# Running both rounds of a recurrent scan layer together: two alternating chains to level 63, then one chain over 64 images

## The reference, cut to what matters

```
for ci, ni, nm, nc in spiral:                 # 1024 steps
    local = g[:, ci, :]
    neigh = (g[:, ni, :] * nm).sum(axis=1) / nc     # up to four neighbours
    u     = concat([local, neigh])                  # 256 values
    y     = tanh(u @ w1 + b1) @ w2 + b2             # 256 hidden units, one number
    g[:, ci, :] = local + y * w_y
```

## Time and profile before

| | us |
|---|---|
| median of 3 runs | 5175.27 (5174.68 to 5177.31) |
| the profiled execution | 5175.03 |
| its span, first to last instruction | 5173.2 |
| PE busy | 4980.8 (96%) |
| VectorE busy | 3493.7 (68%) |
| ScalarE busy | 2927.9 (57%) |
| GpSimd busy | 1018.0 (20%) |
| mean granted clock of TensorE | 0.976 |

### The profile page before, as it was taken

One profiled execution on the slowest core, in us unless ns is written; L12 is line 12 of the kernel. 1 busy time (PEld: TensorE's weight loads), 2 busy tenths in 40 slices (PEclk: granted clock), 3 DMA queues, 4 the chain that ended last, 5 costly groups with the idle time before them and its releaser, 6 DMA issues.

```text
span 5173.2 us, 57594 instructions
## 1 busy us (share of the span) xinstructions
PE 4980.8 (96%) x18384; PEld 2468.8 (48%) x18384; DVE 3493.7 (68%) x6954; ACT 2927.9 (57%) x5457; POOL 1018.0 (20%) x3424
## 2 busy tenths in 40 slices
PE   8998998899999999999999999999999998998997
PEld 3565466344444444444444444444444443565466
DVE  6885886666666666666666666666666656885886
ACT  2222222677777777777777777777777762222222
POOL 4432441011111111111111111111111113432441
PEclk9998998899999999999999999999999999998998
DMA  7653331111111111111111111111111107653331
GB/s 167 93 84 59 47 47 34 38 41 41 41 39 40 41 41 41 41 41 41 41 41 41 41 41 41 41 41 41 41 41 41 41 29 162 93 86 59 47 47 34
DMA packets 373022, 273.22 MB, mean 53 GB/s; under 512 B 338672, under 2 KB 339952, under 8 KB 372720
## 3 DMA queue, kind: packets, MB, share of 16 engines
q1 hardware_dynamic: 372720, 269.54, 22.2%
HBM read 135.29 MB, written 134.22 MB: 52 GB/s over the span
## 4 chain that ended last, share of the span: by engine, by line
PE 91%; DVE 4%; ACT 3%; DMA 1%; issue 1%; POOL 0%; SPq 0%; DVEq 0%; POOLq 0%; ACTq 0%
PE psum L809 35%; PE psum L762 11%; PE psum L782 8%; PE psum L745 8%; PE psum L755 8%; PE psum L844 5%; PE psum L831 5%; PE psum L795 5%; PE psum L859 3%; PE psum L820 3%; ACT hidden L690 2%; DVE near L585 1%; DVE near L562 1%; DVE near L564 1%; POOL near L449 0%
## 5 line engine op out<-in xcount | busy, mean ns | idle before, releaser
L809 PE MATMUL psum<-probs,v 128*128 128x512 f32 x4096 | 1966.9, 603 | 1.3 <-DVE x L653 1.3
L611 DVE TENSOR_REDUCE top<-psum 128x1 f32<-128x1024 f32 x1024 | 1253.5, 1224 | 996.9 <-PE psum L795 996.9
L697 ACT ACTIVATE probs<-psum 128x512 f32<-128x512 f32 x2048 | 1110.3, 594 | 453.4 <-PE psum L782 449.4
L702 ACT ACTIVATE psum<-psum,top 128x1024 f32<-128x1024 f32 x1024 | 1113.0, 1087 | 354.5 <-DVE top L611 354.4
L690 ACT ACTIVATE hidden<-psum,b_col 128x160 f32<-128x160 f32 (+15 forms) x976 | 457.6, 492 | 1296.6 <-PE psum L755 1280.6
L809 PEld LDWEIGHTS psum<-probs,v 128*128 128x128 f32 x4096 | 718.2, 190 | 764.7 <-issue 509.1
L449 POOL TENSOR_TENSOR near<-arena 128x32 f32<-128x32 f32 (+9 forms) x1440 | 597.2, 444 | 1102.2 <-PE psum L755 984.8
L762 PE MATMUL psum<-hidden,w2wy 128*128 128x160 f32 (+14 forms) x1952 | 606.1, 435 | 54.7 <-ACT hidden L690 41.4
L755 PE MATMUL psum<-near,w_sum 128*128 128x160 f32 (+14 forms) x1952 | 583.9, 423 | 60.3 <-POOL near L449 33.6
L745 PE MATMUL psum<-arena,w_own 128*128 128x32 f32 (+15 forms) x2192 | 583.4, 395 | 34.4 <-DMA arena<-x_cells 18.5
L461 POOL TENSOR_TENSOR ratio<-shrink,total 128x8 f32<-128x8 f32 x128 | 26.0, 203 | 2896.8 <-ACT shrink L713 2896.8
(11 more groups left out here) (64 smaller groups left out, 3359.6 us busy)
## 6 DMA issues: line engine op xcount, KB each, us to landing
x<-layer_out SPq DMA_DIRECT2D x128, 512.0 KB, 3.2
layer_out<-x SPq DMA_DIRECT2D x128, 512.0 KB, 2.6
arena<-x_cells SPq DMA_DIRECT2D x6, 1920.0 KB, 19.0
layer_out<-arena SPq DMA_DIRECT2D x6, 1920.0 KB, 17.0
arena<-layer_out SPq DMA_DIRECT2D x6, 1920.0 KB, 18.2
y_cells<-arena SPq DMA_DIRECT2D x6, 1920.0 KB, 16.9
arena<-x_cells SPq DMA_DIRECT2D x4, 2000.0 KB, 19.0
layer_out<-arena SPq DMA_DIRECT2D x4, 2000.0 KB, 15.9
```

The costliest lines, as they stand in the source:

```text
L611: nc.vector.reduce_max(top[i % 2][:, m:m + 1], rows_ps[m % 2][:], AX_X, negate=True).then_inc(row_max, 1)
L697: nc.scalar.activation(probs[u % PROBS][:], keys_ps[u % 2], ACT.Exp).then_inc(probs_ready, 1)
L702: nc.scalar.activation(rows_ps[m % 2][:], rows_ps[m % 2][:], ACT.Exp, bias=top[i % 2][:, m:m + 1], accum_out=total[i % 2][:, m:m + 1]).the ...
L809: nc.tensor.matmul(mix_ps, v[i % 2][:, tile(t)], probs[u % PROBS][:], start=(m == 0), stop=(m == MT - 1)).then_inc(mixed, 1)
```

## The change

Both rounds of a layer are one pass. To level 63 (`JOIN` = 64) there are two streams, A (images 0 to 31) and B (32 to 63), whose levels alternate on every engine; from level 64 there is one stream, BOTH, with 64 images. Each stream has its own semaphores. A and B have one PSUM buffer each for the pre-activations and one for the steps; BOTH alternates between two. The steps of A and B gain a wait for the update of the level before.

The arena has 64 images but only 528 cells: 16 ending cells and the first 32 stay for good, and a window of 480 cells is refilled. The chunks are now at most 96 cells: first levels 0, 2, 8, 14, 20, 27, 34, 43, 53, 65, 80, 101. Chunks 0 to 5 and the ending cells are loaded at the start. Chunks 6 to 11 take places whose earlier tenants must have been stored and read for the last time, which is after levels 13, 26, 33, 40, 40 and 49; they are first read at levels 27, 36, 46, 58, 73 and 94. Every load and store is made twice, for A and for B. For the second scan layer A's first loads are issued in attention after job 116 (`EARLY`), B's at its end.

`near` and `hidden` are twice as large and share their memory with attention's `v` and `probs`; attention starts and ends with a wait for that. The three `scan(n)` in the diff are, in order, those of GpSimd, VectorE and TensorE. The first image load of attention waits for all stores of images 0 to 31, which now end with the layer.

```diff
+JOIN = 64
+A, B, BOTH = range(3)
+SPAN = {A: range(JOIN), B: range(JOIN), BOTH: range(JOIN, LEVELS)}
+PICTURES = {A: slice(0, IMAGES), B: slice(IMAGES, BATCH), BOTH: slice(0, BATCH)}
+CHUNK = 96
+WINDOW = 5 * CHUNK
...
-    arena = sb("arena", [P, IMAGES, CELLS])
+    arena = sb("arena", [P, BATCH, ARENA])
+    shared = [sb(f"shared{n}", [P, BATCH * WIDE]) for n in range(4)]
...
+        def load(n, g, k):
+            for e in earlier_tenants(k):
+                sp.wait_ge(stored[g][e], 16 * (n + 1))
+                wait_level(g, n, max(LAST_READ[chunk_cells(e)]))
...
+            first_loads(0, A)
             load_scan_weights(1)
+            first_loads(0, B)
             load_heads()
-            for r in range(GROUPS):
-                scan(r, r + 1 < GROUPS)
+            follow(0)
...
+                if j == EARLY:
+                    first_loads(1, A)
...
+        def scan(n):
+            for lv in range(LEVELS):
+                for c in streams_at(lv):
+                    late_sums(n, c, lv)
...
+        def scan(n):
+            for c in (A, B):
+                sums(n, c, 1)
+            for lv in range(JOIN - 1):
+                for c in (A, B):
+                    add_steps(n, c, lv + 1)
+                    update(n, c, lv)
+                    if lv + 2 < JOIN:
+                        sums(n, c, lv + 2)
+            sums(n, BOTH, JOIN)
+            add_steps(n, BOTH, JOIN)
+            for c in (A, B):
+                update(n, c, JOIN - 1)
+            for lv in range(JOIN, LEVELS):
+                if lv + 1 < LEVELS:
+                    sums(n, BOTH, lv + 1)
+                    add_steps(n, BOTH, lv + 1)
+                update(n, BOTH, lv)
...
+        def steps(n, c, lv):
+            if c != BOTH:
+                positive(pe, updated[c], levels_done(n, c, lv - 1))
...
+        def scan(n):
+            for c in (A, B):
+                own_products(n, c, 0)
+                near_products(n, c, 0)
+            for lv in range(JOIN):
+                for c in (A, B):
+                    steps(n, c, lv)
+                    if lv + 1 < JOIN:
+                        own_products(n, c, lv + 1)
+                        near_products(n, c, lv + 1)
+            own_products(n, BOTH, JOIN)
+            for lv in range(JOIN, LEVELS):
+                near_products(n, BOTH, lv)
+                steps(n, BOTH, lv)
+                if lv + 1 < LEVELS:
+                    own_products(n, BOTH, lv + 1)
```

More of the change, by code:

```diff
@@ L68, in wavefront @@
     order = sorted(level, key=lambda c: (c in ending, level[c], ring[c]))
[L69 to L73, removed]
+    return rank, level, ending, order
+RANK, LEVEL, ENDING_CELLS, ORDER = levels_of_cells()
@@ new lines, with chunk_levels, chunk_cells @@
+LEVELS = max(LEVEL.values()) + 1
+STARTS = [sum(LEVEL[c] < lv and c not in ENDING_CELLS for c in ORDER) for lv in range(LEVELS + 1)]
+OWN_LEVEL = [LEVEL[c] for c in ORDER]
+CHUNK = 96
+WINDOW = 5 * CHUNK
+def chunk_levels():
+    first = [0, 2]
+    for lv in range(2, LEVELS):
+        if STARTS[lv + 1] - STARTS[first[-1]] > CHUNK and lv > first[-1]:
+            first.append(lv)
+    return first + [LEVELS]
+CHUNKS = chunk_levels()
+ENDING = len(CHUNKS) - 1
+def chunk_cells(k):
+    return slice(STARTS[-1], CELLS) if k == ENDING else slice(STARTS[CHUNKS[k]], STARTS[CHUNKS[k + 1]])
@@ L120, in wavefront @@
         edges.append([(n, k, count) for count, n, k, _, _ in ops[EDGE]])
[L121 to L139, removed]
+    grid = np.array([y * SIDE + x for y, x in ORDER])
+    return grid, ends, sums_late, sums_old, sums_new, steps, edges, first_read, last_read
+GRID, ENDS, SUMS_LATE, SUMS_OLD, SUMS_NEW, STEPS, EDGES, FIRST_READ, LAST_READ = wavefront()
 def level_size(lv):
     return STARTS[lv + 1] - STARTS[lv] + (ENDS[lv] is not None)
-def chunk_cells(k):
-    return slice(STARTS[-1], CELLS) if k == ENDING else slice(STARTS[CHUNKS[k]], STARTS[CHUNKS[k + 1]])
 def positive(engine, semaphore, value):
@@ L589, in update @@
[L589 to L600 removed]
+                for e in STREAMS if c == BOTH else (c,):
+                    if lv - 2 in SPAN[e]:
+                        dve.wait_ge(updated[e], levels_done(n, e, lv - 2))
@@ new lines, in update @@
+        def update(n, c, lv):
+            dve.wait_ge(step_ready[c], levels_done(n, c, lv))
+            for o, w, place in own_parts(lv):
+                own = arena[:, PICTURES[c], place:place + w]
+                ins = nc.vector.scalar_tensor_tensor(own, columns(step(c, lv), c, lv, o, w), b2wy[n][:], own,
+                                                     ALU.add, ALU.add)
+            ins.then_inc(updated[c], 1)
+        def scan(n):
[12 more added lines that the diff above has]
+            for lv in range(JOIN, LEVELS):
@@ L673, in _ @@
         prepare_scan(0)
-        for r in range(GROUPS):
-            scan(r)
+        scan(0)
         prepare_heads()
@@ L889, in _ @@
         pe.wait_ge(out_ready, 2 * JOBS)
-        for r in range(GROUPS, 2 * GROUPS):
-            scan(r)
+        scan(1)
 def build(nc, t):
```

353 lines of the change are left out of this document (182 added, 171 removed).

## The result

The changed kernel takes **4949.8 us** (median of 4 runs, 4948.88 to 4950.95) against 5175.6 us of the kernel before; the ratio is 0.956, 95% interval 0.9547 to 0.958. The forecast was 4916, its range 4870 to 4995. The gain is 225.8 us where 259 were forecast.

A forecast was written before the change was run, and what follows sets the result against it. TensorE looks 96% busy, but the prediction saw time lost in scan waits, narrow levels and gaps. Terms 37 - 49.5 - 42 - 206 + 2 - 1 = -259.5 took 5175.0 to 4916 us; range 4870 to 4995.

The forecast's parts named there:

- What bounds the kernel: Whole kernel: TensorE's 96% busy hides waits within scan levels; narrow levels and the gap between rounds lose time, attention stays.
- a): Levels 64 to 121 run once over 64 images instead of twice over 32: 200 us a layer, gain 206.
- I take the rows of equal columns: Merged levels: a level of w cells is priced by the period of an old level of 2w cells.
- b): Gap between the two rounds of each scan layer disappears: gain 49.5 us.
- c): First layer's start: level 1 waits for the second stream's third load, starting at about 69.6 instead of 32.92: cost 37.
- d): Second layer's start: B's loads land 1 us sooner than the present 29; early loads in attention cost nothing: -1.
- e): Levels 1 to 63 as two alternating chains: the wait for tanh goes, 256.5 for 266.9 us, gain 42.
- f): Refill and hand-over to attention: refills off the path, four short stores replace two, +2 us; kernel end 0.
- Refill stalls: Rival, wide levels: second stream's loads or small descriptors hold them up too, three stalls a layer: 5036 us; chance 0.05.
- Merged levels bound by VectorE as a whole: Rival, merged levels: VectorE's operations take twice the time for twice the elements, 233 for 199 us: 4984; chance 0.10.
- Mutual exclusion: Rival, levels 1 to 63: VectorE and GpSimd exclude each other, +100 x 4 us if fully serial: 5318, slower; chance 0.03.
- the second rival: Merged levels: VectorE bounds them if its operations take twice the time, 4984 us; chance 0.10.

The follow-up runs named there:

- third_addition: Changed kernel with every step addition of the merged levels beyond the first two left out of the computation: 4936.5 us, -13.3 against the changed kernel.
- align: Changed kernel with only the chunks' places in the arena moved by one or two cells each: 4937.8 us, -12.0 against the changed kernel.
- load_order: Changed kernel; in the first layer both streams' chunk 0, ending cells and chunk 1 load first, the second layer's weights last: 4921.7 us, -28.1.
- no_alternation: Changed kernel with levels 0 to 63 of stream A run first, then those of B, then the merged levels: 4992.2 us, +42.4.
- combined_early: Changed kernel with wait order, load order, chunk places and shorter last stores changed, plus B's second-layer first loads mostly issued during attention job 124: 4870.7 us.

## Why the prediction was right, point by point

- **What bounds the kernel**: right. The gains came from the scan, from narrow levels and from gaps, none from attention.
- **a)** The mechanism was right, the term was mis-sized: 200 a layer forecast, 211.2 measured. "I take the rows of equal columns" holds at 7 cells (4.75 forecast and measured) and not below. By sizes, forecast and measured sums are 38.0 and 39.2 at 7 cells, 33.4 and 35.0 at 6, 46.5 and 50.0 at 5, 33.0 and 37.1 at 4, 21.8 and 24.3 at 3, 19.2 and 21.0 at 2; the 1.75 for ending cells is not in these. The failing step is that an old level of equal columns had two additions, a merged one from level 92 on has three, and I added 0.15 for that at 3 cells only; third_addition prices one at about 0.25. The 6-cell levels also met unlucky places (align, 1.7 to 3.3 a layer), and the order of the waits cost 0.03 to 0.09 in most levels from 91 on. With two additions and lucky places 5 cells still took 3.70 for 3.58 and 4 cells 3.14 for 3.00; these 0.12 to 0.14 a level stay unexplained.
- **b)** Right: 49.5, no idle stretch at mid-layer.
- **c)** Right, and load_order shows its cause: 38.2 measured for 37, 28 of which are only issue order.
- **d)** Right: 29.0. The early loads in attention cost nothing, attention being 3364.2 for 3364.0. no_alternation (10.7 us without B) and combined_early (19.5) show what most of those 29 us are: the wait for B's three loads.
- **e)** 46.5 for 42. The three groups of sizes took 113.6, 64.1 and 76.5 a stream where 113.9, 65.0 and 77.5 were forecast. At 9 cells a turn takes 2.97 to 3.01 in the plain levels, below the 3.15 to 3.25 forecast, and 3.18 only in the mean with the dearer ones. The forecast's sum of the old chain, 266.9, stands 1.0 above the 265.9 of the trace: the forecast of 256.5 was worth 38, so the gain was missed by some 9, not 4. "What goes is the wait for tanh" fits the rows: from the neighbour products to the steps it is 1.79 here, 1.88 in the earlier trace rows and 1.99 in no_alternation.
- **f)** Failed: costs of 8.1 and 9.5 where 2 and 0 stood. The step counted four short stores as if bytes decided; instead twice as many runs, half of them with an end that is no multiple of 32 bytes, took 22.4 us from the last update to the end for nearly the bytes that took 12.9.
- **Rivals.** Refill stalls: none, no PE wait for `arena` after level 1. Merged levels bound by VectorE as a whole (4984): false, VectorE is busy 165 of 211 us; but its third addition is on the path at the narrow end, a small part of that rival. Mutual exclusion: false as a rival for the time, but it is there in single instructions. The prediction took 230 us for VectorE where the earlier trace rows have 213, so the overlap that it found in the kernel before is 66 and not 83. In the changed kernel VectorE is busy 425.8 and GpSimd 241.1 of 508.4 us, and the sums of busy time are those of two rounds before (425.1 and 238.0). But an instruction that is held up counts as busy. These are the same sums of GpSimd and VectorE in 6-cell levels, where they start apart and where they start together:

```profile
615.95 1.12 POOL L520 TENSOR_TENSOR shared<-arena 128x192 f32<-128x192 f32 x2 [3.15 <-PE psum L847]
...
620.19 1.50 POOL L520 TENSOR_TENSOR shared<-arena 128x192 f32<-128x192 f32 x2 [3.12 <-PE psum L847]
```

```profile
620.19 1.12 DVE L641 SCALAR_TENSOR_TENSOR shared<-arena,b2wy,shared 128x384 f32<-128x384 f32 x1
...
624.09 0.68 DVE L641 SCALAR_TENSOR_TENSOR shared<-arena,b2wy,shared 128x384 f32<-128x384 f32 x1
```

In levels 1 to 63 a GpSimd sum of 32 elements takes 0.24 to 0.32 us alone or beside VectorE's additions from PSUM, and up to 0.87 (before) and 0.80 (after) beside its sums with two inputs in SBUF. That agrees with the exclusion that the Trainium skill states ("SBUF — State Buffer", section "SBUF: two separate sides"). It was there before the change as after it, and GpSimd's busy sum grew by 3 us only (238.0 to 241.1) with two chains.
- **The range.** That it holds is in part luck: it was built from c, e, f and the second rival, with no room for a by itself. As c and e came close to their forecasts, their room was free for a's miss.

## What to carry to other kernels

Merge two chains where their levels are so narrow that hand-overs and fixed parts take much of the period (here under 256 columns each), and alternate them where they are wider, if a merged level would only equal a pair; take the period of a merged level from a row with equal columns only if it also has the same number of instructions on the leg that ends last. Before costing a refill at nothing, follow the issue queue to the load that the first instruction of the last stream needs. Count the transfers at the end of a stage in runs, and look where each run begins and ends.

## What the runs showed of the hardware that was not expected

- **Writes to HBM in short runs.** The same 8192 runs took 7.7 us to land each transfer at 256 bytes from byte 3840, and 13.8 us at 264 bytes from byte 3832; the rate of the latter falls from 225 to about 130 GB/s only after some 3 us. Pairs of stores of 1.5 MB landed in 10.4, 16.8 or 21.4 us with two, one or no end of their runs on a multiple of 32 bytes.
- **Operands of TensorE.** Four own products of 384 columns took 1.29 or 1.79 us by the place of the 6-cell runs modulo 16 bytes, and moving chunks by one, two or four cells gained 12.0 us in all.
- **Order of two waits.** With the wait that is met last directly in front of the instruction, VectorE's addition started 0.28 us after the own products; with another, long met, between them, 0.20 to 0.22. That was worth 8.2 us.
- **VectorE and GpSimd.** A GpSimd sum of 32 elements took about 0.30 us, and up to 0.87 beside VectorE's sums with two inputs in SBUF, before the change as well as after it.
